# Pair activations computed token by token, multiplied on GpSimd into the summed weights

## Chip, core and metric

The kernel runs on one core of a Trainium2 chip. The metric is device time in microseconds. The engines named here: TensorE (PE, with its weight loads PEld), VectorE (DVE), ScalarE (ACT) and GpSimd (POOL). Each takes its instructions in order and waits on semaphores.

## The reference

Two layers on x of shape (16, 128, 128): 16 tiles of 128 tokens with 128 features, all float32. Each layer is a conditioning part and a feed-forward part with a residual. The change lies in the feed-forward part of layer 0, a product-key memory of 1024 experts:

```python
sim = einsum('pbnhd,hkpd->pbnhk', q, keys)
sx, ix = top_k(sim[0], 8); sy, iy = top_k(sim[1], 8)
all_scores = sx[..., :, None] + sy[..., None, :]
scores, pk = top_k(all_scores, 8)
h = gelu(einsum('bnd,bnhkd->bnhk', x, down_embed[indices]))
h = softmax(scores) * h
out = einsum('bnhk,bnhkd->bnd', h, up_embed[indices])
```

Layer 1 is a mixture of 8 experts of three matrices (256 hidden) and then a mixture of 8 experts of two matrices (512 hidden), on the 128 features of each token.

## The kernel before, in words

The memory is computed densely. For a tile of 128 tokens, `pair_scores` (GpSimd, L401) forms for each of 8 heads all 32x32 sums of key scores; ScalarE masks them (L989) and exponentiates them (L995); `add_weights` (VectorE, L1392) adds the heads, each with its softmax factor, into one array W of 128 tokens x 1024 experts. The activation of every expert for every token, gelu(x . down), is computed by `expert_inputs`: TensorE (L663) multiplies eight blocks of 128 experts, with the block of `downT` as the stationary operand, so that experts lie on partitions; ScalarE (L1003) applies gelu into `act_of[t]`. TensorE's `weights_T` (L673) transposes W into PSUM in eight steps (L681). VectorE's `weigh` (L1479) multiplies these by the activations on their way into `PT` (L1489). `peer_out` (L684) multiplies PT with the `up` matrix, and `add_peer` (L1408) makes the output `x2s` of the layer.

Tiles 0 and 1 are done in another way (TensorE sums their heads, L783); tiles 2 to 15 as told.

Work is staged in turns of two tiles: turn g handles the even tile 2g and the odd tile 2g+1 of the memory, together with layer 1 for the two tiles before. A turn has 16 slots, and each engine's order of instructions in a slot is written out by hand. In slots 4 to 11 layer 1's first mixture runs, one expert a slot: TensorE `hidden1(e+1)`, `outputs1(e-2)`, `hidden2(e)`; VectorE evicts `hidden1(e)` with its ReLU (L1398) and ScalarE `hidden2(e)` (L1041). TensorE's `hidden2(e)` waits for VectorE's `hidden1(e)`, and its `hidden1(7)` waits for VectorE's `hidden1(6)` (L732). The gate of the mixture is worked out on VectorE in slots 4 to 6 (L1432 to L1477; the copy L1462 is `keep_two`). The second mixture runs in slots 12 to 15 and 0 to 3.

The heads of `add_weights` are spread over VectorE's slots by a table: `SUMS` (L1571) in turns 2 to 7, `SUMS_1` (L1573) in turn 1. Entry 1 to 7 is a head of the even tile, 9 to 15 a head of the odd one. Head 0 needs no sum. A sum waits for its predecessor's semaphore. TensorE's `weights_T` for the even tile stands in slot 10, for the odd tile in slot 1 of the next turn. GpSimd's `pair_scores` of head h for the tile after next reuses the buffer of head h and waits for its sum (`h_w`). The buffers of the activations, `G[0]` and `G[1]`, alternate between even and odd tiles.

Of the kernel before, what the change touches and what calls it, by code (L numbers as in the profile page):

```python
# [21 lines left out]
ALU = mybir.AluOpType  # L22
# [3 lines left out]
P = 128  # L26
# [56 lines left out]
def program(nc, xtok, xT, pA, pL, pC, pR, p8, wq, wqT, down, up, w1, w2, w3, f1, f2, out):  # L83
# [7 lines left out]
    with ExitStack() as ctx:  # L91
        def sb(name, shape, dt=F32):
            return ctx.enter_context(nc.sbuf_tensor(name, shape, dt))

        def sem(name):
            return ctx.enter_context(nc.semaphore(name))
# [3 lines left out]
        x1T_all = sb("x1T_all", [P, TOK])  # L100
        downT = sb("downT", [P, NK * NK])
# [81 lines left out]
        W = [W_both[:, 1024 * a:1024 * a + 1024] for a in range(2)]  # L183
# [5 lines left out]
        PT = sb("PT", [P, 1024])  # L189
# [11 lines left out]
        act_of = [HF[n][:, :, :].rearrange("p a n -> p (a n)") for n in range(2)] + [G[n % 2] for n in range(2, B)]  # L201
# [17 lines left out]
        banks = ctx.enter_context(nc.psum_tensor("banks", [P, 8, 512], F32))  # L219

        def bank(n, a=0, b=512):
            return banks[:, n, a:b]
# [25 lines left out]
        topk = sem("topk")  # L248

        t_top, t_ez, t_zs, t_rz = (sem("t_" + n) for n in ("top", "ez", "zs", "rz"))  # L250
        t_Hp, t_G = sem("t_Hp"), sem("t_G")


        t_dg, t_W, t_Tp, t_PT, t_x2p, t_x2, t_xst, t_ssq, t_trp, t_x2T = (
            sem("t_" + n) for n in ("dg", "W", "Tp", "PT", "x2p", "x2", "xst", "ssq", "trp", "x2T"))

        h_S, h_L, h_E, h_w = sem("h_S"), sem("h_L"), sem("h_E"), sem("h_w")
# [15 lines left out]
        def wait(eng, s, value):  # L273

            if not isinstance(value, int) or value > 0:
                eng.wait_ge(s, value)
# [4 lines left out]
        def cols(ap, i, n=P):  # L281
            return ap[:, ds(i * n, n)] if not isinstance(i, int) else ap[:, i * n:(i + 1) * n]

        def tile_of(ap, t):
            if isinstance(t, int):
                return ap[:, t, :]
            return ap[:, ds(t, 1), :].rearrange("p a n -> p (a n)")
# [40 lines left out]
        def _(pool):  # L328
# [60 lines left out]
            def pair_scores(t, a, h):  # L389

                if h == 0:
                    pool.wait_ge(t_simr, t + 1)
                    if t == 0:
                        pool.wait_ge(pe_norm, len(NORM_PE))
                if 2 <= t < 4:
                    pool.wait_ge(t_W, 8 * (t - 2) + h + 1)
                elif h == 0:
                    wait(pool, h_E, 8 * (t - 2) + 1)
                else:
                    wait(pool, h_w, 7 * (t - 4) + h)  # L400
                pool.tensor_tensor(  # L401
                    S[a][h].rearrange("p (i j) -> p i j", i=NK),
                    sim[a][:, h, :].unsqueeze(2).broadcast_to([P, NK, NK]),
                    sim[a][:, PH + h, :].unsqueeze(1).broadcast_to([P, NK, NK]),
                    ALU.add).then_inc(h_S, 1)

            def keep_x2(t, a):
                pool.wait_ge(t_x2, t + 1)
                pool.tensor_copy(tile_of(x_all, t), x2s[a][:, :]).then_inc(t_xst, 1)  # L409
# [8 lines left out]
            def turn(g, peer, new, more=True):  # L418
                t = 2 * g

                def root():
                    pool.wait_ge(g_msq, g)
                    pool.tensor_tensor(rms[:, :], msq[:, :], mhalf[:, 0:2], ALU.pow).then_inc(g_rms, 1)

                if g == 1:
                    root()
                if peer:
                    for h in range(7):
                        pair_scores(t + 1, 1, h)
                if new and g > 1:  # L430
                    keep_x2(t - 1, 1)
                    root()
                if not peer:
                    return
                pair_scores(t + 1, 1, 7)
                if more:
                    for h in range(8):
                        pair_scores(t + 2, 0, h)
                keep_x2(t, 0)

            for t in range(2):
# [2 lines left out]
            for h in range(3):  # L444
                pair_scores(2, 0, h)
            keep_x2(0, 0)
            for h in range(3, 8):
                pair_scores(2, 0, h)
            keep_x2(1, 1)
            for g in range(1, NG - 1):  # L450
                turn(g, True, True)
            turn(NG - 1, True, True, more=False)
            turn(NG, False, True, more=False)


        @block.tensor
        def _(pe):
            def mm(o, l, r, start=True, stop=True):
                return pe.matmul(o, l, r, start=start, stop=stop)  # L459
# [203 lines left out]
            def expert_inputs(t, a, c):  # L663

                if c == 0 and t != 2:
                    pe.wait_ge(t_G, t)
                    wait(pe, t_PT, t - 1)
                b = 4 + c if t == 2 else c
                for k in range(4):
                    m = mm(bank(b, P * k, P * k + P), cols(downT, 4 * c + k), cols(x1T_all, t))  # L670
                m.then_inc(t_Hp, 1)

            def weights_T(t, a):  # L673
                pe.wait_ge(h_w, 7 * t - 7)
                if a == 1:
                    pe.wait_ge(t_G, min(t + 2, B))
                else:
                    pe.wait_ge(e_r2, 4 * t - 2)
                pe.wait_ge(t_PT, t)
                for c in range(8):  # L680
                    m = pe.transpose(bank(c // 4, P * (c % 4), P * (c % 4) + P), W[a][:, P * c:P * c + P], ident[:, :])  # L681
                m.then_inc(t_Tp, 1)
# [100 lines left out]
            def weighted(t, h):  # L783
# [9 lines left out]
                m.then_inc(t_W, 1)  # L793

            expert_inputs(1, 1, 0)
            expert_inputs(1, 1, 1)
            expert_inputs(2, 0, 0)
            expert_inputs(2, 0, 1)
            key_scores(1, 1)
# [16 lines left out]
            def turn(g, peer, new, old, more=True):  # L816
                t, G1, G2 = 2 * g, g - 1, g - 2
                late = new and g > 1
                for s in range(16):
# [14 lines left out]
                    if s == 1 and late:  # L834
                        weights_T(t - 1, 1)
# [22 lines left out]
                    if s == 10 and peer:  # L858
                        weights_T(t, 0)
# [34 lines left out]
        def _(act):  # L894
# [107 lines left out]

            def expert_inputs(t, a):  # L1003
                act.wait_ge(t_Hp, 2 * t + 2)
                if t > 2:
                    act.wait_ge(t_PT, t - 1)
                b = 4 if t == 2 else 0
                act.activation(act_of[t], banks[:, b:b + 2, :].rearrange("p c n -> p (c n)"),
                               ACT.Gelu_apprx_tanh).then_inc(t_G, 1)
# [45 lines left out]
            act.wait_ge(pe_norm, NORM_PE.index("weff0") + 1)  # L1055
            act.activation(weff[:, 0:256], bank(2, 0, 256), ACT.Copy).then_inc(act_norm, 1)
            expert_inputs(0, 0)
            act.wait_ge(pe_norm, NORM_PE.index("sim_bias") + 1)
            act.activation(sim_bias[:, :], bank(7), ACT.Copy).then_inc(act_norm, 1)
            expert_inputs(1, 1)  # L1060
            expert_inputs(2, 0)
            load_table(ACT.Exp, 1)
            exp_top(0, 0)
# [85 lines left out]
        def _(v):  # L1149
# [328 lines left out]

            def weigh(t, a):  # L1479

                b = 0
                if t < 2:
                    b = 2 + 2 * t
                    v.wait_ge(t_W, 8 * t + 8)
                else:
                    v.wait_ge(t_Tp, t - 1)
                v.wait_ge(t_G, t + 1)
                wait(v, t_x2p, t)
                v.tensor_tensor(PT[:, :], banks[:, b:b + 2, :].rearrange("p c n -> p (c n)"), act_of[t],  # L1489
                                ALU.mult).then_inc(t_PT, 1)  # L1490

            def diagonals(t, a, b):
# [22 lines left out]
            def add_expert(Gn, n):  # L1515
# [15 lines left out]
                for a in range(2):  # L1531
# [26 lines left out]
            top_pairs(0)  # L1558
            thresholds(2, 0)
            weigh(0, 0)  # L1560
            add_peer(0, 0)
            key_sums(3, 1)
            top_keys_of(3, 1)
            pair_sums()
            top_pairs(1)
            thresholds(3, 1)
            weigh(1, 1)
            add_peer(1, 1)
            top_sums(2, 0)

            SUMS = {0: [1], 2: [2], 4: [3], 6: [4], 7: [5], 8: [6], 9: [7], 10: [9, 10], 11: [11, 12], 12: [13],  # L1571
                    13: [14], 14: [15]}
            SUMS_1 = {0: [1], 6: [2, 3], 7: [4], 8: [5], 9: [6, 7], 10: [9, 10], 11: [11, 12], 12: [13], 13: [14], 14: [15]}  # L1573
            ADDS = {6: 0, 7: 1, 8: 2, 9: 3, 10: 4, 11: 5, 14: 8, 15: 9}
# [2 lines left out]
            def turn(g, peer, new, old, more=True):  # L1577
                t, G1, G2 = 2 * g, g - 1, g - 2
                late = new and g > 1
                sums = SUMS if late else SUMS_1  # L1580
                slots = list(range(16)) if g != 1 else [4, 5, 0, 6, 1, 7, 2, 8, 3, 9, 10, 11, 12, 13, 14, 15]
                for s in slots:
# [41 lines left out]
                    if s == 2 and late:  # L1624
                        weigh(t - 1, 1)
# [92 lines left out]
```

## Time and profile before

| | us |
|---|---|
| median of 3 runs | 799.05 (798.32 to 799.29) |
| the profiled execution | 798.92 |
| its span, first to last instruction | 797.1 |
| TensorE busy | 762.6 (96%) |
| VectorE busy | 548.3 (69%) |
| ScalarE busy | 574.2 (72%) |
| GpSimd busy | 315.6 (40%) |
| mean granted TensorE clock | 0.989 of full |

The attention part of layer 0 runs until about 145 us, a stretch of set-up and the first tiles until 228, turn 1 until about 276, turns 2 to 7 until about 700, and the rest is the end of layer 1. A busy share is an average over these. Times in a timeline are from the span's start; consecutive matmuls of TensorE overlap in it, so the time that one takes of the engine is read from its start to the start of the next.

### The profile page before, as it was taken

What the parts mean: (1) busy time and instruction counts of PE and PEld (TensorE: products, weight loads), DVE (VectorE), ACT (ScalarE), POOL (GpSimd) and SP (SyncE); (2) the same over time, 40 slices, a digit from 0 to 9 for tenths busy, and PEclk for the clock granted to TensorE, in tenths of its full rate; (3) what the DMA queues carried; (4) which work ended last, traced back from release to release, by engine and by line L of the source; (5) the groups of instructions that cost most, each with busy time, mean ns of one, the idle gap of its engine ahead of it and who ended that gap; (6) DMA issues with size and microseconds to landing.
All of it is one profiled execution on the core that took longest, in us unless ns stands there. A gap on an engine that the chain in (4) does not pass through costs nothing.

```text
span 797.1 us, 14545 instructions
## 1 busy us (share of the span) xinstructions
PE 762.6 (96%) x5186; PEld 681.3 (85%) x5186; DVE 548.3 (69%) x1479; ACT 574.2 (72%) x985; POOL 315.6 (40%) x230
## 2 busy tenths in 40 slices
PE   4999999998976999999999999999999999999998
PEld 3888888887964789899998998999998899899887
DVE  3577667559459967977896697779769765843522
ACT  2667667529978688978887897789789788653343
POOL 2122222049997364516635460763546171000000
PEclk9999999998998999999999999999999999999999
DMA  8930000000000000000000000000000000000000
GB/s 308 340 101 2 1 2 2 1 2 0 2 0 1 2 1 5 4 2 1 8 1 1 1 8 1 1 8 1 2 2 7 1 1 8 1 1 4 5 1 7
DMA packets 11015, 16.85 MB, mean 21 GB/s; under 512 B 664, under 2 KB 6976, under 8 KB 10688
## 3 DMA queue, kind: packets, MB, share of 16 engines
q1 hardware_dynamic: 10944, 15.93, 6.2%
q8 instruction: 42, 0.69, 0.4%
q14 instruction: 29, 0.24, 0.1%
HBM read 14.88 MB, written 1.05 MB: 20 GB/s over the span
## 4 chain that ended last, share of the span: by engine, by line
PE 89%; DVE 6%; issue 3%; ACT 2%; DMA 1%; POOL 0%; DVEq 0%; SPq 0%; ACTq 0%; POOLq 0%
PE banks L459 82%; PE banks L498 4%; PE banks L681 2%; DVE W_both L1392 1%; ACT region L989 1%; DVE acc L1537 1%; DMA region<-in_pC 1%; PE banks L514 0%; DVE W_both L1195 0%; DVE HF L1398 0%; ACT region L995 0%; PE banks L713 0%; DVE pairs L1356 0%; DVE top_keys L1351 0%; DVE PT L1489 0%
## 5 line engine op out<-in xcount | busy, mean ns | idle before, releaser
L401 POOL TENSOR_TENSOR region<-sim 128x1024 f32<-128x1024 f32 x128 | 260.8, 2066 | 99.7 <-DVE top_keys L1349 63.2
L1051 ACT ACTIVATE HF<-banks,lpack 128x256 f32<-128x256 f32 x256 | 105.6, 480 | 55.4 <-PE banks L459 54.5
L989 ACT ACTIVATE region<-region,neg_thr 128x1024 f32<-128x1024 f32 x128 | 143.8, 1153 | 0.0
L1392 DVE SCALAR_TENSOR_TENSOR W_both<-region,rz_rel,W_both 128x1024 f32<-128x1024 f32 x98 | 137.7, 1405 | 1.7
L459 PE MATMUL banks<-HF,w_sb 128*128 128x256 f32 x512 | 124.4, 387 | 7.5 <-DVE HF L1398 7.4
L459 PEld LDWEIGHTS banks<-f_sb,HF 128*128 128x128 f32 x1024 | 123.7, 192 | 3.4
L995 ACT ACTIVATE region<-region,dtop 128x1024 f32<-128x1024 f32 x114 | 125.4, 1142 | 0.0
L459 PE MATMUL banks<-f_sb,HF 128*128 128x128 f32 x1024 | 124.5, 275 | 0.0
L459 PE MATMUL banks<-cT,f_sb 128*128 128x256 f32 x512 | 122.7, 382 | 0.1
L459 PEld LDWEIGHTS banks<-HF,w_sb 128*128 128x128 f32 x512 | 95.2, 194 | 19.8 <-DVE HF L1398 8.5
L459 PEld LDWEIGHTS banks<-cT,f_sb 128*128 128x128 f32 x512 | 92.1, 190 | 16.3 <-issue 2.9
L1041 ACT ACTIVATE H<-banks,lpack 128x256 f32<-128x256 f32 x128 | 53.4, 470 | 49.5 <-PE banks L459 49.5
L459 PE MATMUL banks<-region 128*128 128x128 f32 (+7 forms) x478 | 73.8, 400 | 8.6 <-DMA region<-in_pC 5.3
L409 POOL COPY x_all<-x2s 128x128 f32<-128x128 f32 x16 | 11.6, 723 | 163.7 <-DVE x2s L1408 163.6
L1398 DVE TENSOR_SCALAR HF<-banks,lpack 128x256 f32<-128x256 f32 x128 | 55.8, 476 | 23.9 <-PE banks L459 23.6
L459 PEld LDWEIGHTS banks<-w_sb,H 128*128 128x128 f32 x512 | 66.1, 192 | 6.7 <-ACT H L1041 2.8
L459 PE MATMUL banks<-w_sb,H 128*128 128x128 f32 x512 | 68.7, 277 | 2.1 <-DVE acc L1537 1.0
L1537 DVE SCALAR_TENSOR_TENSOR acc_f<-banks,cw,acc_f 128x128 f32<-128x128 f32 x112 | 34.0, 345 | 50.9 <-PE banks L459 50.1
L459 PE MATMUL banks<-x2T,w_sb 128*128 128x256 f32 x256 | 67.7, 388 | 0.0
L459 PEld LDWEIGHTS banks<-region 128*128 128x128 f32 (+3 forms) x478 | 51.7, 199 | 16.3 <-issue 7.9
L459 PE MATMUL banks<-region,G_both 128*128 128x104 f32 x512 | 62.8, 276 | 0.0
L459 PEld LDWEIGHTS banks<-region,G_both 128*128 128x128 f32 x512 | 59.7, 192 | 0.0
(165 smaller groups left out, 1010.7 us busy)
## 6 DMA issues: line engine op xcount, KB each, us to landing
w_sb<-in_w SPq DMA_DIRECT2D x1, 2048.0 KB, 12.9
f_sb<-in_f SPq DMA_DIRECT2D x1, 2048.0 KB, 15.8
region<-in_wq SPq DMA_DIRECT2D x1, 1024.0 KB, 9.3
region<-in_wqT SPq DMA_DIRECT2D x1, 1024.0 KB, 11.4
w_sb<-in_w SPq DMA_DIRECT2D x1, 1024.0 KB, 8.5
out_x<-acc_f SPq DMA_DIRECT2D x16, 64.0 KB, 1.6
region<-in_pA SPq DMA_DIRECT2D x1, 796.5 KB, 4.3
x1T_all<-in_xT SPq DMA_DIRECT2D x1, 768.0 KB, 8.3
```

The costliest lines, as they stand in the source:

```text
L401: pool.tensor_tensor(S[a][h].rearrange("p (i j) -> p i j", i=NK), sim[a][:, h, :].unsqueeze(2).broadcast_to([P, NK, NK]), sim[a][:, PH + h ...
L409: pool.tensor_copy(tile_of(x_all, t), x2s[a][:, :]).then_inc(t_xst, 1)
L459: return pe.matmul(o, l, r, start=start, stop=stop)
L498: m = pe.transpose(bank(g // FG, P * (g % FG), P * (g % FG) + P), D[q][:, P * g:P * g + P], A("ident"))
L681: m = pe.transpose(bank(c // 4, P * (c % 4), P * (c % 4) + P), W[a][:, P * c:P * c + P], ident[:, :])
L989: act.activation(S[a][h], S[a][h], ACT.Prelu, bias=neg_thr[t % 4][:, h:h + 1], alpha=STEEP).then_inc(h_L, 1)
L995: act.activation(W[a] if h == 0 and t > 1 else S[a][h], S[a][h], ACT.Exp, bias=dtop[t % 4][:, h, 7:8]).then_inc(h_E, 1)
L1041: m = act.activation(H2[e % 2][:, n, :], bank(H2_BANK[e], 256 * n, 256 * n + 256), ACT.Relu, bias=L("b2", 2 * e + n, 2 * e + n + 1))
L1051: m = act.activation(HF[e % 2][:, f, :], bank(2 + b, 256 * (f % 2), 256 * (f % 2) + 256), ACT.Gelu_apprx_tanh, bias=L("bf", 4 * e + f, 4 * ...
L1392: v.scalar_tensor_tensor(W[a], S[a][h], rz_rel[a][:, h:h + 1], W[a], ALU.mult, ALU.add).then_inc(h_w, 1)
L1398: m = v.tensor_scalar(H1[e % 2][:, n, :], bank(H1_BANK[e], 256 * n, 256 * n + 256), L("b1", 2 * e + n, 2 * e + n + 1), 0.0, ALU.add, ALU.max)
L1537: m = v.scalar_tensor_tensor(dst[:, a, :], y, weight, base, ALU.mult, ALU.add)
```

## The change

`expert_inputs` on TensorE takes, for tiles 2 to 15, the tile of x as the stationary operand and 512 columns of `downT` as the moving one: two products, tokens on partitions. The gelu output then has the layout of W. A new step `pair_products` on GpSimd multiplies it into W in place, once the sums are complete, and signals a new semaphore `t_P`. `weights_T` waits for that, and VectorE's `weigh` for these tiles is a copy from PSUM to PT. ScalarE's gelu waits for the GpSimd product of the tile that last used its buffer. On GpSimd the product of the odd tile stands after four of the `pair_scores` of the next odd tile, the one of the even tile between `pair_scores` 6 and 7 of the next even tile. In `SUMS` the even tile's heads 4, 5, 6 and 7 move from slots 6, 7, 8, 9 to slots 5, 6, 7, 8. `SUMS_1` is as it was.

```diff
+            def pair_products(t, a):
+
+                pool.wait_ge(h_w, 7 * t - 7)
+                pool.wait_ge(t_G, t + 1)
+                pool.tensor_tensor(W[a], W[a], act_of[t], ALU.mult).then_inc(t_P, 1)
+
...
                 if peer:
-                    for h in range(7):
+                    for h in range(4):
+                        pair_scores(t + 1, 1, h)
+                if new and g > 1:
+                    pair_products(t - 1, 1)
+                if peer:
+                    for h in range(4, 7):
                         pair_scores(t + 1, 1, h)
...
                 if more:
-                    for h in range(8):
+                    for h in range(7):
                         pair_scores(t + 2, 0, h)
+                pair_products(t, 0)
+                if more:
+                    pair_scores(t + 2, 0, 7)
                 keep_x2(t, 0)
...
-                for k in range(4):
-                    m = mm(bank(b, P * k, P * k + P), cols(downT, 4 * c + k), cols(x1T_all, t))
+                if t > 1:
+                    m = mm(bank(b), cols(x1T_all, t), downT[:, 512 * c:512 * c + 512])
+                else:
+                    for k in range(4):
+                        m = mm(bank(b, P * k, P * k + P), cols(downT, 4 * c + k), cols(x1T_all, t))
                 m.then_inc(t_Hp, 1)
 
             def weights_T(t, a):
-                pe.wait_ge(h_w, 7 * t - 7)
+                pe.wait_ge(t_P, t - 1)
...
-                if t > 2:
+                if t == 3:
                     act.wait_ge(t_PT, t - 1)
+                elif t > 3:
+                    act.wait_ge(t_P, t - 3)
...
-                b = 0
-                if t < 2:
-                    b = 2 + 2 * t
-                    v.wait_ge(t_W, 8 * t + 8)
-                else:
+                wait(v, t_x2p, t)
+                if t > 1:
                     v.wait_ge(t_Tp, t - 1)
+                    v.tensor_copy(PT[:, :], banks[:, 0:2, :].rearrange("p c n -> p (c n)")).then_inc(t_PT, 1)
+                    return
...
-            SUMS = {0: [1], 2: [2], 4: [3], 6: [4], 7: [5], 8: [6], 9: [7], 10: [9, 10], 11: [11, 12], 12: [13],
+            SUMS = {0: [1], 2: [2], 4: [3], 5: [4], 6: [5], 7: [6], 8: [7], 10: [9, 10], 11: [11, 12], 12: [13],
```

## Rows read from the trace of the kernel before

**Rows 1.** Stretches: us, busy (instructions) of each engine, PEclk, DMA share, GB/s.
```profile
250.00:262.00 12.00, 10.10 (x32) 7.86 (x31) 11.97 (x24) 6.71 (x10) 9.57 (x5) 0.64 0.00 0
350.39:420.90 70.51, 70.47 (x461) 63.89 (x461) 55.79 (x158) 58.91 (x97) 34.89 (x19) 1.00 0.01 3
```

**Rows 2.** Waits of TensorE, 230 to 790: total us, times, longest.
```profile
PE banks L459 <- DVE HF L1398: 7.4, 3, 4.4
```

**Rows 3.** Timeline of TensorE: start, us, instruction, count; `key_scores` and `expert_inputs`.
```profile
353.96 1.02 PE L459 MATMUL banks<-weff,x1T_all 128*128 128x512 f32 x2
354.82 1.89 PE L459 MATMUL banks<-cT,f_sb 128*128 128x256 f32 x8
...
358.33 1.95 PE L459 MATMUL banks<-x1T_all,downT 128*128 128x128 f32 x16
360.12 1.89 PE L459 MATMUL banks<-cT,f_sb 128*128 128x256 f32 x8
```

**Rows 4.** Groups of VectorE by form: busy us, mean ns, idle before.
```profile
L1489 DVE TENSOR_TENSOR PT<-banks,G_both 128x1024 f32<-128x1024 f32 x14 | 17.1, 1219 | 1.8 <-PE banks L681 1.8
...
L1339 DVE COPY sim<-banks 128x512 f32<-128x512 f32 x1 | 0.7, 692 | 1.2 <-PE banks L459 1.2
```

**Rows 5.** Timeline of TensorE, turn 3: transposes, `hidden2(4)`, `hidden1(7)`, transposes.
```profile
371.74 1.04 PE L681 MATMUL banks<-ident,W_both 128*128 128x128 f32 x8
...
399.37 1.89 PE L459 MATMUL banks<-HF,w_sb 128*128 128x256 f32 x8
...
404.80 1.03 PE L459 MATMUL banks<-x2T,w_sb 128*128 128x256 f32 x4
...
409.02 1.09 PE L681 MATMUL banks<-ident,W_both 128*128 128x128 f32 x8
```

**Rows 6.** Timeline of VectorE, turn 3: `hidden1(3)`, copy, sums, `hidden1(4)`, `hidden1(6)`.
```profile
391.72 0.88 DVE L1398 TENSOR_SCALAR HF<-banks,lpack 128x256 f32<-128x256 f32 x2
392.51 0.82 DVE L1462 COPY picked<-best 128x4 f32<-128x4 f32 x1
...
394.79 1.28 DVE L1392 SCALAR_TENSOR_TENSOR W_both<-region,rz_rel,W_both 128x1024 f32<-128x1024 f32 x1
395.98 0.87 DVE L1398 TENSOR_SCALAR HF<-banks,lpack 128x256 f32<-128x256 f32 x2
...
400.50 1.84 DVE L1392 SCALAR_TENSOR_TENSOR W_both<-region,rz_rel,W_both 128x1024 f32<-128x1024 f32 x1
402.39 0.88 DVE L1398 TENSOR_SCALAR HF<-banks,lpack 128x256 f32<-128x256 f32 x2
...
404.13 1.28 DVE L1392 SCALAR_TENSOR_TENSOR W_both<-region,rz_rel,W_both 128x1024 f32<-128x1024 f32 x1
```

**Rows 7.** Timeline of GpSimd, turn 3; in brackets the idle time before.
```profile
356.88 14.62 POOL L401 TENSOR_TENSOR region<-sim 128x1024 f32<-128x1024 f32 x7 [9.05 <-DVE top_keys L1349]
...
382.93 10.37 POOL L401 TENSOR_TENSOR region<-sim 128x1024 f32<-128x1024 f32 x5
396.15 1.91 POOL L401 TENSOR_TENSOR region<-sim 128x1024 f32<-128x1024 f32 x1 [2.84 <-DVE W_both L1392]
399.36 1.91 POOL L401 TENSOR_TENSOR region<-sim 128x1024 f32<-128x1024 f32 x1 [1.29 <-DVE W_both L1392]
```

**Rows 8.** Timeline of ScalarE, turn 3: the masks of heads 2 to 4, odd tile.
```profile
375.27 3.22 ACT L989 ACTIVATE region<-region,neg_thr 128x1024 f32<-128x1024 f32 x3
```

**Rows 9.** Timelines of turn 1: TensorE, VectorE and GpSimd.
```profile
265.71 1.09 PE L681 MATMUL banks<-ident,W_both 128*128 128x128 f32 x8
265.73 1.92 POOL L401 TENSOR_TENSOR region<-sim 128x1024 f32<-128x1024 f32 x1 [1.16 <-DVE W_both L1392]
266.88 3.24 DVE L1392 SCALAR_TENSOR_TENSOR W_both<-region,rz_rel,W_both 128x1024 f32<-128x1024 f32 x2
...
271.31 1.13 PE L459 MATMUL banks<-w_sb,H 128*128 128x128 f32 x8 [1.00 <-DVE acc L1537]
...
276.16 0.44 PE L772 MATMUL banks<-ident,acc 128*128 128x128 f32 x2 [0.87 <-DVE acc L1537]
```

More of the change, by code:

```diff
@@ L250, in program @@
         t_top, t_ez, t_zs, t_rz = (sem("t_" + n) for n in ("top", "ez", "zs", "rz"))
-        t_Hp, t_G = sem("t_Hp"), sem("t_G")
+        t_Hp, t_G, t_P = sem("t_Hp"), sem("t_G"), sem("t_P")
         t_dg, t_W, t_Tp, t_PT, t_x2p, t_x2, t_xst, t_ssq, t_trp, t_x2T = (
@@ L1479, in weigh @@
             def weigh(t, a):
-                b = 0
-                if t < 2:
-                    b = 2 + 2 * t
-                    v.wait_ge(t_W, 8 * t + 8)
-                else:
+                wait(v, t_x2p, t)
+                if t > 1:
                     v.wait_ge(t_Tp, t - 1)
+                    v.tensor_copy(PT[:, :], banks[:, 0:2, :].rearrange("p c n -> p (c n)")).then_inc(t_PT, 1)
+                    return
+                v.wait_ge(t_W, 8 * t + 8)
                 v.wait_ge(t_G, t + 1)
-                wait(v, t_x2p, t)
-                v.tensor_tensor(PT[:, :], banks[:, b:b + 2, :].rearrange("p c n -> p (c n)"), act_of[t],
+                v.tensor_tensor(PT[:, :], banks[:, 2 + 2 * t:4 + 2 * t, :].rearrange("p c n -> p (c n)"), act_of[t],
                                 ALU.mult).then_inc(t_PT, 1)
```

## The prediction, as made before the change was run

> **What bounds the kernel now.** I read the stretches first [rows 1]: in one whole steady turn, 350.39 to 420.90, TensorE is busy for 70.47 of 70.51 us at full clock. So in the steady turns nothing costs time unless TensorE gets more work or has to wait, and nothing brings time unless TensorE gets less work. Only 250 to 262, in turn 1, looks different: TensorE idles and its granted clock is 0.64. The table of waits says where TensorE idles after the start-up [rows 2]: mostly for VectorE's "HF" evictions, the ReLUs of `hidden1` (L1398), three times, 7.4 us in all, of which I find every one in turn 1. TensorE is therefore the bound, and the engine nearest to becoming it is VectorE. That makes the timelines of one steady turn, TensorE beside VectorE beside GpSimd, the place to work in; I use turn 3. Turn 2 and turns 4 to 6 repeat it at a shift of 70.5 us.
>
> **1. Two 512-column products for eight 128-column ones.** In a steady turn 16 such instructions (one tile's `expert_inputs`; a float32 product is two instructions) run from 358.33 to the next start at 360.12, 1.79 us a tile. A 512-column product, `key_scores`, runs from 353.96 to 354.82, 0.86 us, so a tile will take 1.72 us [rows 3]. Saved: 0.07 us for each of 14 tiles (2 to 15), about 1.0 us, all on the bounding engine. The arithmetic itself is unchanged, so more is hard to see: below it lies only 0, if the saving is an edge effect.
>
> The Trainium skill, "TensorE: Matmul & The Clock Gate", section "Wait — 56ns, not 53.3ns?", puts a fixed 2.5 ns on each matmul beyond its columns. By it 14 x 12 instructions fewer would give back an estimated 0.4 us in place of my 1.0. The rows give the larger figure, and I take theirs.
>
> **2. VectorE copies instead of multiplying.** The multiplication into PT takes 1219 ns for 1024 columns. The nearest row for a copy out of PSUM is 692 ns for 512 columns [rows 4]; twice that is 1.38 us, and less the fixed part about the same 1.2 us. So VectorE gives up nothing. That work is not shortened, only copied.
>
> **3. GpSimd multiplies.** The product reads and writes 1024 columns of SBUF. Its nearest row is `pair_scores`, 1.91 us for 128x1024 with two inputs [rows 7]. It adds 14 x 1.91 = 27 us to an engine that is 40% busy, but what counts is when.
> - Odd tile: GpSimd runs seven `pair_scores` from 356.88 for 14.62 us. Four of them and the product end at about 367.4. TensorE's transposes of that tile start at 371.74 [rows 5, 7]. Slack 4 us: free. Three `pair_scores` come 2 us later, and their batch ends at 373.4; ScalarE's three instructions for heads 2 to 4 begin at 375.27, so head 4, done at about 369.5, is wanted at 377.3 [rows 8].
> - Even tile: the product is queued between `pair_scores` 6 and 7 and waits for the last sum. Today the last sum ends at 404.13 + 1.28 = 405.4; TensorE transposes at 409.02 [rows 5, 6]. Even unmoved, 405.5 + 1.9 = 407.4 would be in time by 1.6 us. So the new wait is hidden in steady turns, up to a product of 3.5 us.
>
> **4. The even tile's sums, one slot earlier (turns 2 to 7).** The sum for head 4 now stands at the end of slot 5, in front of `hidden1(3)`, not in slot 6. Two things in the rows price that.
>
> First, VectorE instructions with two SBUF inputs, and its tiny SBUF-to-SBUF copies, stand still while a GpSimd instruction runs. The copy of 4 columns (L1462) at 392.51 takes 0.82 us and ends at 393.33; GpSimd's run of five that began at 382.93 ends at 393.30. The sum at 400.50 takes 1.84 instead of 1.28 us; GpSimd's instruction beside it, from 399.36, ends at 401.27 [rows 6, 7]. PSUM evictions such as L1398 are not held up.
>
> Second, the moved sum lands in that same run. It would issue at about 391.7, where `hidden1(3)` issues today, be held until 393.30, and let `hidden1(3)` start at 394.3 (1.0 to 1.1 us after GpSimd is done, as `hidden1(6)` at 402.39 after 401.27). That is 2.65 us later, of which 1.46 us is standing still. Its end releases GpSimd's `pair_scores` for head 4, 394.4 to 396.4, and L1462, issued at 395.1, is held until 396.4: 0.5 us more than today. The rest of the spacing repeats today's (the sum at 400.50, held by 0.6 us, has its counterpart in the sum for head 7). So `hidden1(4)` and `hidden1(6)` both start about 3.05 us later than today.
>
> What was the cover? `hidden1(4)` ends today at 396.85 and TensorE takes it up in the eight instructions at 399.37: cover 2.5 us, short by 0.6. `hidden1(6)` ends at 402.39 + 0.88 = 403.27 and TensorE's `hidden1(7)`, which by L732 waits for it, starts at 404.80: cover 1.5 us, short by 1.57, in which the first 0.6 is contained. After that VectorE waits for TensorE again, so nothing is added by the end of the turn. So 1.57 us a turn. GpSimd's run of 10.37 us comes five times, in turns 2 to 6; turn 7 has none (no further tile to score): 5 x 1.57 = 7.9 us. Bounds for a turn: 0.1 (if the moved sum is not held, the delay is 1.6 against 1.5) and 2.2 (if it is held by another full instruction's remainder). I take 1.57, for the row of L1462 shows something held in just that place.
>
> The Trainium skill, "SBUF — State Buffer", section "SBUF: two separate sides", calls the SBUF port pair that VectorE and GpSimd share an exclusive lock held for the whole instruction; if bandwidth were shared instead, the moved sum would be slowed but not stopped. The row of L1462 agrees with the lock, since four columns can't take 0.82 us at half speed.
>
> **5. Turn 1.** There the sums are not moved. TensorE's transposes start at 265.71, right when the last sum is done; so does a GpSimd instruction of 1.92 us that waited for that sum, at 265.73 [rows 9]. The product takes that place, and TensorE waits until 267.7: 2.0 us. TensorE idles later in the same turn for 1.00 and 0.87 us for VectorE, so of the 2.0 us at least 0.1 to 0.2 stays. But GpSimd's last `pair_scores` moves behind the product, until 269.6, and holds the second of the two sums that start at 266.88 (today only the first is held, 3.24 us for both). That adds up to 1.9 us to VectorE's chain, which is the late one there. I take 1.6 us; bounds 0.2 and 2.0.
>
> **The sum.** Profiled execution 798.92 us (span 797.1, 1.8 around it): 798.92 - 1.0 + 7.9 + 1.6 = 807.4 us. The median of the runs shown, 799.05, lies 0.13 above this execution, inside what I can tell.
>
> **The rivals.**
> - **The sums are not held, or the cover is wider than I read it** (24%). Then only part 1 and turn 1 stay: 798.92 - 1.0 + 0.2 to 1.6, 798.1 to 799.5, with up to 0.2 a turn 800.5. For it: VectorE catches up within each turn, and 1.5 us of cover is close to what one plain sum needs. Against: the held copy in the same place. This is the case on the other side, not slower, and what decides is whether the head-4 sum issues before GpSimd's fifth instruction has ended.
> - **Held once only** (15%): the moved sum is held for part of an instruction, or the copy behind it isn't: 0.2 to 1.0 us a turn, 800.7 to 804.5.
> - **TensorE's clock falls in turn 1** (7%). Ahead of the stretch at 0.64 TensorE had idled 4.4 us at once, its longest wait. With the new 2 us at 265.7 a second fall could come; if the 8 to 10 us of work behind it ran at half speed, 4 to 8 us more than my sum: 811 to 815. Against: the new idle is less than half as long.
> - **The change pays more on TensorE than the rows show** (8%): 168 weight loads go as well, and if the stalls stay out and each tile gave 0.25 us, 14 x 0.25 = 3.5 us: 796.
>
> **How the numbers follow.** My forecast holds 46%: 804.5 to 809.5. Range 799.0 to 809.5: outside it lie the clock (7%), the larger gain (8%) and the low edge of the first rival (3%). Less than 0.2% (1.6 us, about what a measurement of this kernel can tell from no change) is the first rival, 24%. Slower: 46 + 15 + 7 = 68%. Faster: 8%.
>
> **What would show it.** Right: in turns 2 to 6 TensorE has idle time ended by VectorE HF L1398, some 1.5 us a turn; the period of a turn grows from 70.5 to about 71.9; the head-4 sum takes about 2.7 us and L1462 about 1.3. GpSimd's products take 1.9 us, and both steady transposes wait for nothing. In turn 1 the transposes start 2 us after the last sum. Each `expert_inputs` tile takes 1.72 us. Wrong: a steady turn of 70.4 us with a head-4 sum of 1.3 us kills part 4; a product of over 3.5 us would turn the new wait into the bound; a 512-column product far from 0.86 us would upset part 1.

## The result, and the profile after

The changed kernel takes 811.64 us (median of 4 runs, 808.53 to 811.80) against 799.17 us for the kernel before: a ratio of 1.0144, 95% interval 1.0115 to 1.0174. It is slower, as forecast, but by 12.5 us where 8.5 were forecast, and outside the range that ended at 809.5. The profiled execution is 811.69 us, its span 809.9, again 1.8 us around it.

Line numbers have moved: TensorE's L459 is L473, its transposes L681 are L698; VectorE's sums L1392 are L1411, the evictions L1398 are L1417, the copy L1462 is L1481; GpSimd's product is L411.

The page of the changed kernel, part 1, is the first thing to read:

```profile
PE 767.4 (95%) x5018; PEld 669.0 (83%) x5018; DVE 563.2 (70%) x1479; ACT 575.0 (71%) x985; POOL 349.1 (43%) x244
```

168 fewer products and loads on TensorE, and yet it is busy for longer (762.6 before). A busy time that rises while the work falls suggests that part of it ran at a lower clock; the stretches below show where. Then who TensorE waited for from 230 on (total us, times, longest), which answers [rows 2]:

```profile
PE banks L473 <- DVE HF L1417: 12.5, 13, 4.4
PE banks L473 <- ACT cT L1044: 2.5, 2, 2.1
PE banks L698 <- POOL W_both L411: 2.5, 1, 2.5
```

Three waits for VectorE's evictions have become 13: ten new ones, two in each of turns 2 to 6. The product is waited for once, in turn 1. Of the two waits for `cT` one, of 2.05 us, is new and in turn 1; the other, of 0.5 us near the end, was there before. Stretches of the changed kernel (us, busy of each engine, PEclk), three in and around turn 1 and one a whole steady turn, which answer [rows 1]:

```profile
250.00:262.00 12.00, 10.12 (x33) 7.79 (x32) 11.93 (x25) 6.77 (x10) 9.86 (x5) 0.64 0.00 0
262.00:276.00 14.00, 11.49 (x66) 10.15 (x65) 13.58 (x14) 7.34 (x12) 7.11 (x3) 0.87 0.00 1
276.00:288.00 12.00, 9.95 (x47) 7.47 (x47) 6.45 (x20) 9.24 (x16) 1.28 (x1) 0.86 0.00 0
357.64:429.58 71.94, 70.87 (x438) 61.78 (x437) 58.24 (x158) 59.03 (x97) 39.52 (x21) 1.00 0.01 3
```

A steady turn has grown from 70.51 to 71.94 us with TensorE idle for 1.1 of them. And in turn 1 the clock is below full in two stretches more; before, both had 1.00. The chain of work that ended last puts the difference in place. Its long TensorE pieces begin each turn at the same instruction, in the changed kernel:

```profile
285.58 17.84 PE banks L473 x104
...
357.64 17.71 PE banks L473 x104
...
645.37 16.85 PE banks L473 x102
...
714.88 14.28 PE banks L473 x96
```

In the kernel before, the same four stand at 279.88, 350.39, 632.42 and 702.07. So 5.7 us are lost ahead of turn 2 (0.3 of them ahead of turn 1), (645.37 - 285.58) - (632.42 - 279.88) = 7.25 us in turns 2 to 6, -0.14 in turn 7, nothing after: 12.8 us, the whole difference of the two spans. Where the 0.3 us ahead of turn 1 come from stays open.

### The profile page after: what moved, and what is told of

Its sections match the earlier page's. It is cut to its first block, busy times and chain, and to the rows that moved or that the text cites. A ratio compares the mean times of both kernels' runs of the same rounds, so it can differ in the third digit from the quotient of the medians.

```text
span 809.9 us, 14237 instructions
## 1 busy us (share of the span) xinstructions
PE 767.4 (95%) x5018; PEld 669.0 (83%) x5018; DVE 563.2 (70%) x1479; ACT 575.0 (71%) x985; POOL 349.1 (43%) x244
## 4 chain that ended last, share of the span: by engine, by line
PE 75%; DVE 14%; issue 7%; ACT 2%; DMA 1%; POOL 0%; DVEq 0%; SPq 0%; ACTq 0%; POOLq 0%
PE banks L473 68%; PE banks L512 4%; DVE W_both L1411 3%; DVE HF L1417 3%; PE banks L698 2%; DVE acc L1555 1%; DVE picked L1481 1%; ACT region L1006 1%; ACT region L1012 1%; DVE prob L1464 1%; DMA region<-in_pC 1%; PE banks L528 0%; DVE W_both L1214 0%; DVE pairs L1375 0%; DVE acc_f L1555 0%
## 5 line engine op out<-in xcount | busy, mean ns | idle before, releaser
L401 POOL TENSOR_TENSOR region<-sim 128x1024 f32<-128x1024 f32 x128 | 256.1, 2026 | 96.1 <-DVE top_keys L1368 66.5
L1411 DVE SCALAR_TENSOR_TENSOR W_both<-region,rz_rel,W_both 128x1024 f32<-128x1024 f32 x98 | 151.3, 1543 | 1.7
L473 PE MATMUL banks<-HF,w_sb 128*128 128x256 f32 x512 | 125.5, 389 | 9.7 <-DVE HF L1417 9.6
L473 PEld LDWEIGHTS banks<-f_sb,HF 128*128 128x128 f32 x1024 | 123.7, 192 | 3.4
L473 PE MATMUL banks<-f_sb,HF 128*128 128x128 f32 x1024 | 124.5, 275 | 0.0
L473 PE MATMUL banks<-cT,f_sb 128*128 128x256 f32 x512 | 124.2, 386 | 0.1
L473 PEld LDWEIGHTS banks<-HF,w_sb 128*128 128x128 f32 x512 | 95.7, 195 | 23.1 <-DVE HF L1417 11.7
L473 PEld LDWEIGHTS banks<-cT,f_sb 128*128 128x128 f32 x512 | 93.7, 192 | 19.4 <-issue 5.9
L473 PE MATMUL banks<-region 128*128 128x128 f32 (+7 forms) x478 | 73.8, 400 | 8.9 <-DMA region<-in_pC 5.6
L1417 DVE TENSOR_SCALAR HF<-banks,lpack 128x256 f32<-128x256 f32 x128 | 55.6, 475 | 23.4 <-PE banks L473 23.3
L473 PEld LDWEIGHTS banks<-w_sb,H 128*128 128x128 f32 x512 | 67.0, 195 | 5.8 <-ACT H L1060 1.8
L473 PE MATMUL banks<-x2T,w_sb 128*128 128x256 f32 x256 | 68.2, 391 | 2.9 <-DVE HF L1417 2.9
L473 PE MATMUL banks<-w_sb,H 128*128 128x128 f32 x512 | 69.6, 280 | 1.1 <-DVE acc L1552 0.8
L473 PEld LDWEIGHTS banks<-region 128*128 128x128 f32 (+3 forms) x478 | 51.7, 199 | 16.5 <-issue 7.9
L473 PE MATMUL banks<-region,G_both 128*128 128x104 f32 x512 | 62.8, 276 | 0.0
L473 PEld LDWEIGHTS banks<-region,G_both 128*128 128x128 f32 x512 | 59.7, 192 | 0.0
```

Of the source, the lines that this page charges most:

```text
L401: pool.tensor_tensor(S[a][h].rearrange("p (i j) -> p i j", i=NK), sim[a][:, h, :].unsqueeze(2).broadcast_to([P, NK, NK]), sim[a][:, PH + h ...
L1411: v.scalar_tensor_tensor(W[a], S[a][h], rz_rel[a][:, h:h + 1], W[a], ALU.mult, ALU.add).then_inc(h_w, 1)
L1417: m = v.tensor_scalar(H1[e % 2][:, n, :], bank(H1_BANK[e], 256 * n, 256 * n + 256), L("b1", 2 * e + n, 2 * e + n + 1), 0.0, ALU.add, ALU.max)
```

## Where the steady turns lose 1.4 us each

VectorE in turn 3 of the changed kernel, from the point at which it was priced:

```profile
398.85 2.73 DVE L1411 SCALAR_TENSOR_TENSOR W_both<-region,rz_rel,W_both 128x1024 f32<-128x1024 f32 x1
401.50 0.86 DVE L1417 TENSOR_SCALAR HF<-banks,lpack 128x256 f32<-128x256 f32 x2
402.29 1.31 DVE L1481 COPY picked<-best 128x4 f32<-128x4 f32 x1
...
405.05 1.27 DVE L1411 SCALAR_TENSOR_TENSOR W_both<-region,rz_rel,W_both 128x1024 f32<-128x1024 f32 x1
406.25 0.87 DVE L1417 TENSOR_SCALAR HF<-banks,lpack 128x256 f32<-128x256 f32 x2
```

GpSimd and TensorE beside it, in the same turn (the first GpSimd line is its run of five, the two behind it are the fourth and the fifth of these by themselves):

```profile
390.12 10.37 POOL L401 TENSOR_TENSOR region<-sim 128x1024 f32<-128x1024 f32 x5
...
395.73 2.90 POOL L401 TENSOR_TENSOR region<-sim 128x1024 f32<-128x1024 f32 x1
398.58 1.91 POOL L401 TENSOR_TENSOR region<-sim 128x1024 f32<-128x1024 f32 x1
...
401.65 1.91 POOL L401 TENSOR_TENSOR region<-sim 128x1024 f32<-128x1024 f32 x1 [1.16 <-DVE W_both L1411]
...
412.69 2.36 POOL L411 TENSOR_TENSOR W_both<-W_both,G_both 128x1024 f32<-128x1024 f32 x1 [1.16 <-DVE W_both L1411]
```

```profile
407.17 1.99 PE L473 MATMUL banks<-HF,w_sb 128*128 128x256 f32 x8 [0.45 <-DVE HF L1417]
...
413.45 1.13 PE L473 MATMUL banks<-x2T,w_sb 128*128 128x256 f32 x4 [0.58 <-DVE HF L1417]
...
417.77 1.09 PE L698 MATMUL banks<-ident,W_both 128*128 128x128 f32 x8
```

The head-4 sum takes 2.73 us. It is issued at 398.85, 0.27 us after GpSimd's fifth instruction began, and ends 1.09 us after that instruction, which ends at 400.49. It is this one instruction that it waits for, not the run: the head-3 sum, issued at 395.16 in the same run, took 1.70 us, and there GpSimd's fourth instruction was the one held, 2.90 instead of 1.91 us. The head-4 sum's own end releases GpSimd's next scores at 401.65, and those hold the copy L1481 until 403.6. TensorE then idles in front of `hidden2(4)` and in front of `hidden1(7)`; the brackets say 0.45 and 0.58 us. Start to start it is more: against the spacing of the kernel before, 0.62 us is lost at the first place and 0.74 at the second, and 0.1 behind each (the eight products at 407.17 take 1.83 us to the next start where they took 1.73), 1.57 us in all. The transposes at 417.77 wait for nothing: the product that they need ended at 415.05.

**The moved sums alone.**

```diff
-            SUMS = {0: [1], 2: [2], 4: [3], 6: [4], 7: [5], 8: [6], 9: [7], 10: [9, 10], ...
+            SUMS = {0: [1], 2: [2], 4: [3], 5: [4], 6: [5], 7: [6], 8: [7], 10: [9, 10], ...
```

> The kernel before with the moved sums alone; no product on GpSimd, no 512-column products. Theory A: 1.58 us a turn in turns 2 to 6, period 72.1 us, 799.2 + 7.9 = 807.1 us. Rival B: 799.2 us, period 70.5.

Measured 806.58 us against 799.00, ratio 1.0089 (1.0068 to 1.0109): 7.6 us, with neither a product on GpSimd nor a 512-column one. Its period is 72.07 us, 1.56 more than before: theory A.

**The other way round: the changed kernel with its sums back** (the same two lines, exchanged).

> The changed kernel with one part undone: in turns 2 to 7 the even tile's sums stand in their old slots. Theory A, that the moved sums cost the steady turns 1.58 us in each of turns 2 to 6: the period of a turn falls from 71.93 to 70.37 us, no idle time of TensorE before hidden2(4) and hidden1(7), and about 811.6 - 7.9 = 803.7 us. The product of the even tile then starts after the last sum, 1.3 us later than in the changed kernel, and must still end before TensorE's transposes. Rival B, that the GpSimd products cost the steady turns (VectorE held up by them, or TensorE waiting for them): the period stays above 71.5 and the time at 811.

Measured 806.61 us (803.68 to 807.04), ratio to the kernel before 1.0083 (1.0058 to 1.0107). Both theories missed: the period is 70.97 us where they had 70.37 and over 71.5, so 0.97 us a turn came back, not 1.58. TensorE no longer waits for evictions in steady turns, but it has a new wait for VectorE's additions into `acc`; more of that below.

**How much is standing still, how much is plain work.** Two kernels tell it. One moves a single sum:

```diff
-            SUMS = {0: [1], 2: [2], 4: [3], 6: [4], 7: [5], ...
+            SUMS = {0: [1], 2: [2], 4: [3], 5: [4], 7: [5], ...
```

> The kernel before with one sum moved, head 4 from slot 6 to slot 5; heads 5, 6 and 7 stay. Theory A (the moved sum waits until GpSimd's run of five scores has ended, 1.46 us, and the copy L1462 behind it 0.5 us more): hidden1(4) and hidden1(6) later by about 1.9 us, against a cover of 2.5 and 1.5: stall 0.4 us before hidden1(7) alone, in turns 2 to 6, 2.0 us in all, 801.0 us. Rival D (nothing stands still, only one more sum of 1.2 us lies in front): with one sum moved and one gone from the slot behind, hidden1(4) is where it was, no stall, 799.0 us.

Measured 801.35 us, ratio 1.0030 (1.0020 to 1.0040), period 70.94 us, that is 0.43 us a turn where 0.4 was worked out and the rival had none.

The other keeps all four moved, and shortens GpSimd's run:

```diff
+                n = NK // 2 if t > 3 and a == 0 and h in (2, 3) else NK
                 pool.tensor_tensor(
-                    S[a][h].rearrange("p (i j) -> p i j", i=NK),
-                    sim[a][:, h, :].unsqueeze(2).broadcast_to([P, NK, NK]),
+                    S[a][h][:, 0:n * NK].rearrange("p (i j) -> p i j", i=n),
+                    sim[a][:, h, 0:n].unsqueeze(2).broadcast_to([P, n, NK]),
```

> The kernel before with the four moved sums, and GpSimd's scores for heads 2 and 3 of the even tiles from tile 4 on computed for half of the 1024 pairs only (the other half is left out). GpSimd's run of five then ends before the head-4 sum issues. Theory A: the sum takes 1.3 instead of 2.7 us, hidden1(4) and hidden1(6) are later by 1.2 to 1.6 us, against a cover of 2.5 and 1.5: at most 0.1 us a turn is left, 799.0 to 799.6 us. Rival D (the number of sums in front of the evictions is what costs): the stall stays, 806.6 us.

Measured 798.60 us, period 70.75 us: 0.24 us a turn are left (at most 0.1 was expected), of the 1.56 of the moved sums alone (ratio to the kernel before 0.9994, 0.9984 to 1.0003). VectorE in this kernel:

```profile
390.44 1.27 DVE L1393 SCALAR_TENSOR_TENSOR W_both<-region,rz_rel,W_both 128x1024 f32<-128x1024 f32 x1
391.62 0.87 DVE L1399 TENSOR_SCALAR HF<-banks,lpack 128x256 f32<-128x256 f32 x2
392.41 1.31 DVE L1463 COPY picked<-best 128x4 f32<-128x4 f32 x1
```

GpSimd's run of five ends at 390.21 here, before the sum is issued. The head-4 sum is down from 2.73 to 1.27 us, as many sums stand in front of the evictions as in the moved version, and the stall is nearly gone. The copy is still held, by the scores that the sum releases. So it is the standing still behind a GpSimd instruction, not the number of sums. (That the total is even below the periods' account is turn 1, whose tile 4 is shortened too: turn 2 starts 1.6 us sooner.)

The Trainium skill, "SBUF — State Buffer", section "SBUF: two separate sides", has it that the loser of the shared port pair blocks for the whole instruction of the other. By that rule, the trace agrees: the copy ends with GpSimd's instruction (403.60 and 403.56), the head-4 sum ends 1.09 us after one, most of the 1.27 us that a sum takes by itself, and GpSimd's own fourth instruction is held behind the head-3 sum.

**The 512-column products alone**, in the kernel before:

```diff
-                for k in range(4):
-                    m = mm(bank(b, P * k, P * k + P), cols(downT, 4 * c + k), cols(x1T_all, t))
+                if t > 1:
+                    m = mm(bank(b), cols(x1T_all, t), downT[:, 512 * c:512 * c + 512])
+                else:
+                    for k in range(4):
+                        m = mm(bank(b, P * k, P * k + P), cols(downT, 4 * c + k), cols(x1T_all, t))
```

> The kernel before with the 512-column products alone, for tiles 2 to 15. VectorE still multiplies, but the activations now lie token by token while the transposed weights lie expert by expert, so the pairing of the two is left out of this kernel's result. Theory A: each tile's products take 1.72 instead of 1.79 us, period 70.37 instead of 70.51 us, 1.0 us in all: 799.0 - 1.0 = 798.0 us. Rival: no gain of TensorE at all, 799.0 us and a period of 70.51.

Measured 798.72 us, ratio 0.9997 (0.9987 to 1.0006). The period is 70.37 us, shorter by the 0.14 us a turn of two tiles that was worked out. The medians differ by 0.3 us, and the interval holds both the 1.0 us expected and none; the gain is read from the period in the trace alone.

## Where turn 1 loses 5.4 us

TensorE in the changed kernel, which answers [rows 9]:

```profile
268.43 1.36 PE L698 MATMUL banks<-ident,W_both 128*128 128x128 f32 x8 [2.47 <-POOL W_both L411]
...
271.29 2.51 PE L473 MATMUL banks<-HF,w_sb 128*128 128x256 f32 x8
...
281.71 0.61 PE L473 MATMUL banks<-lpack,cT 128*128 128x8 f32 x4 [2.05 <-ACT cT L1044]
282.17 3.20 PE L473 MATMUL banks<-cT,f_sb 128*128 128x256 f32 x8
```

The two levels of the clock, each in a stretch of its own after its wait:

```profile
269.20:272.40 3.20, 3.20 (x14) 3.02 (x13) 3.10 (x3) 0.00 (x0) 2.02 (x1) 0.50 0.00 0
272.60:282.60 10.00, 7.90 (x50) 6.09 (x49) 7.40 (x15) 7.97 (x11) 1.28 (x1) 1.00 0.00 1
282.80:286.10 3.30, 3.30 (x10) 2.57 (x9) 2.09 (x10) 1.53 (x4) 0.00 (x0) 0.50 0.00 0
```

And ScalarE at the end of the same turn, in the changed kernel and then in the kernel before:

```profile
273.83 0.84 ACT L1060 ACTIVATE H<-banks,lpack 128x256 f32<-128x256 f32 x2 [6.66 <-PE banks L473]
274.56 2.19 ACT L1006 ACTIVATE region<-region,neg_thr 128x1024 f32<-128x1024 f32 x2
276.65 1.14 ACT L1012 ACTIVATE W_both<-region,dtop 128x1024 f32<-128x1024 f32 x1
277.69 2.18 ACT L1012 ACTIVATE region<-region,dtop 128x1024 f32<-128x1024 f32 x2
279.88 1.28 ACT L990 ACT_TABLE_LOAD   x1
...
281.29 0.37 ACT L1044 ACTIVATE cT<-banks 128x256 f32<-128x256 f32 x1
```

```profile
269.46 0.84 ACT L1041 ACTIVATE H<-banks,lpack 128x256 f32<-128x256 f32 x2 [2.55 <-PE banks L459]
...
276.91 0.37 ACT L1025 ACTIVATE cT<-banks 128x256 f32<-128x256 f32 x1
```

Followed down the turn, against the kernel before and net of 0.3 us from ahead of it: the transposes are 2.4 us later (the product takes 2.35 us, not 1.9). `hidden2(7)` is 3.5 us later: between the two the same work took 2.86 instead of 1.82 us, at a lower clock. The products that need cT are 4.1 us later. And the work from there to 287.51 takes 5.80 instead of 4.34 us, again at a lower clock. That is 2.4 + 1.0 + 0.6 + 1.5 = 5.5 us, within 0.1 of what the chain of work gives.

ScalarE is the link that my sum lacks. Its last eviction of the first mixture waits for `hidden2(7)`; behind it stand 7.5 us of masks, exponentials and a table load without a gap, and then the copy of cT, which TensorE waits for. In the kernel before, the same eviction ran at 269.46 and the copy at 276.91, straight behind the same work, and it ended 0.05 us before TensorE took it up at 277.33. The slack of TensorE that I counted on, 1.00 and 0.87 us of waits for VectorE [rows 9], was there and was used up, but it was not the path. VectorE's chain was priced rightly: the two sums behind the product take 5.13 us for 3.24, the 1.9 us foreseen.

**Turn 1 as before, the rest as changed.** Tile 2 keeps its eight products, VectorE's multiplication, and transposes that wait for the sums:

```diff
-                if t > 1:
+                if t > 2:
                     m = mm(bank(b), cols(x1T_all, t), downT[:, 512 * c:512 * c + 512])
...
-                pe.wait_ge(t_P, t - 1)
+                if t == 2:
+                    pe.wait_ge(h_w, 7)
+                else:
+                    pe.wait_ge(t_P, t - 2)
...
-                pair_products(t, 0)
+                if g > 1:
+                    pair_products(t, 0)
```

> The changed kernel with tile 2 alone (turn 1) done as before: eight 128-column products, VectorE multiplies into PT, TensorE's transposes wait for the sums alone. Theory A: turn 1 lost 5.4 us to the product in front of the transposes and to what followed from it (TensorE's clock, ScalarE's late copy of cT); all of it comes back, 811.6 - 5.4 = 806.2 us, and the granted clock of turn 1 after 262 us is full again. Rival C: the loss of turn 1 comes from the rest of the change (other instruction order, start-up), and at most 2.4 us, the bare wait for the product, come back: 809.2 us.

Measured 806.05 us (ratio to the kernel before 1.0083, 1.0066 to 1.0100) against the changed kernel's 811.64, so 5.6 us came back where 5.4 were expected and the rival had 2.4, and the clock from 262 on is full:

```profile
262.00:276.00 14.00, 11.53 (x76) 9.56 (x74) 13.48 (x18) 10.27 (x14) 3.82 (x2) 1.00 0.01 2
276.00:288.00 12.00, 11.82 (x68) 9.67 (x69) 8.37 (x36) 8.70 (x21) 2.89 (x2) 1.00 0.00 0
```

**A shorter product, in the same place.** From the kernel with its sums back (806.61 us):

```diff
-                pool.tensor_tensor(W[a], W[a], act_of[t], ALU.mult).then_inc(t_P, 1)
+                n = 256 if t == 2 else 1024
+                pool.tensor_tensor(W[a][:, 0:n], W[a][:, 0:n], act_of[t][:, 0:n], ALU.mult).then_inc(t_P, 1)
```

> The changed kernel with the sums in their old slots (which ran at 806.6 us), and the product of tile 2 on GpSimd taken over 256 of its 1024 columns (the others are left without it). The wait and its order in every queue stay, its length falls from 2.35 to about 0.6 us. Theory A (turn 1 pays first for the length of TensorE's wait and then again for the clock that falls after it): TensorE waits 0.7 us before the transposes, its clock stays at full speed, and nearly all of turn 1's 5 us come back: 802 us. Rival E (the wait alone, and ScalarE's late copy, no clock): 1.8 us come back, 804.8 us. Rival F (order, not length): 806.6 us.

Measured 803.52 us, with a spread of 801.52 to 805.22 (ratio to the kernel before 1.0056, 1.0039 to 1.0073): by the medians 3.1 us came back, where theory A had 4.6 and rival E 1.8. The trace is of a run of 802.03 us. In it TensorE waits 0.86 us ahead of the transposes, the stretch 262 to 276 is back at full clock, the wait for cT in turn 1 is gone, and turn 2 starts at 280.87 instead of 285.44: 4.6 us for a product of 0.73 instead of 2.35 us, shorter by 1.6. So the length of the wait is what turn 1 pays, and it pays more than the length. How much more varies from run to run: two of the six took 805.2 us, and why they gained less than the one traced, no trace shows.

**Less work on ScalarE**, from the same kernel:

```diff
-                act.activation(W[a] if h == 0 and t > 1 else S[a][h], S[a][h], ACT.Exp,
+                n = 32 if t == 4 and h in (1, 2) else 1024
+                dst = W[a] if h == 0 and t > 1 else S[a][h]
+                act.activation(dst[:, 0:n], S[a][h][:, 0:n], ACT.Exp,
```

> The changed kernel with the sums in their old slots (which ran at 806.6 us), and two of ScalarE's exponentials of turn 1, heads 1 and 2 of tile 4, taken over 32 of 1024 columns (the rest is left out), 2.0 us less work between its last eviction of the first mixture and the copy of cT. Theory A (in turn 1 TensorE's late start reaches cT through ScalarE, which has no slack there): TensorE's wait of 2.05 us for cT goes, and 2.0 us come back, 804.6 us, up to 1.4 more if TensorE's clock then stays up behind it. Rival G (ScalarE's lateness is covered by TensorE's own): 806.6 us.

Measured 803.66 us (803.10 to 804.51; ratio to the kernel before 1.0064, 1.0046 to 1.0082), 2.9 us less for 1.7 us less work (the two exponentials take 0.52 instead of 2.18 us; 2.0 was expected); turn 2 starts at 282.57. TensorE's wait for cT in turn 1 is 0.4 us. Its wait for the product is still 2.4 us and the clock from 262 to 276 still 0.86, but from 276 to 288 it is 1.00:

```profile
262.00:276.00 14.00, 11.55 (x66) 10.16 (x65) 13.58 (x14) 7.18 (x11) 7.10 (x3) 0.86 0.00 1
276.00:288.00 12.00, 11.61 (x65) 8.78 (x65) 8.08 (x23) 9.67 (x21) 1.28 (x1) 1.00 0.01 1
```

So the two waits each have a stretch of lower clock behind them, and each goes with its own wait. ScalarE's lateness and the clock behind it are both real terms, as theory A had it.

## What the moved sums were covering

**Both undone together** (the edits of the two kernels above in one):

> Both of the others together: sums in their old slots and tile 2 done as before; tiles 3 to 15 keep the 512-column products and the product on GpSimd. Theory A: 799.2 minus 13 tiles x 0.07 us = 798.3 us, period 70.37 us. If the GpSimd products cost anything in steady turns (rival B), it is above 799.2.

Measured 801.52 us, ratio 1.0028 (1.0018 to 1.0038): 3.2 us above what I expected, period 70.98 us. VectorE, TensorE and GpSimd in turn 3 of this kernel:

```profile
406.93 4.53 DVE L1415 SCALAR_TENSOR_TENSOR W_both<-region,rz_rel,W_both 128x1024 f32<-128x1024 f32 x2
```

```profile
417.51 0.44 PE L793 MATMUL banks<-ident,acc 128*128 128x128 f32 x2 [0.39 <-DVE acc L1564]
```

```profile
405.15 2.37 POOL L411 TENSOR_TENSOR W_both<-W_both,G_both 128x1024 f32<-128x1024 f32 x1 [1.16 <-DVE W_both L1415]
407.47 2.90 POOL L401 TENSOR_TENSOR region<-sim 128x1024 f32<-128x1024 f32 x1
```

The product is in time for the transposes by itself, as I had said. What I had not asked is who else it stands beside. The two sums of slot 10 now run beside the product and the scores behind it and take 4.53 us instead of 2.66; the additions into `acc` behind them come late, and TensorE's transposes of `acc` wait. With the sums moved, as the change has them, this wait is gone, at the price of the longer stall earlier in the turn.

**One odd sum later**, from that kernel:

```diff
-            SUMS = {..., 9: [7], 10: [9, 10], 11: [11, 12], 12: [13],
+            SUMS = {..., 9: [7], 10: [9], 11: [10, 11], 12: [12, 13],
```

> The kernel with both parts undone (even sums in their old slots, tile 2 as before; it ran at 801.5 us), and in turns 2 to 7 one odd sum moved back by a slot: heads 1, then 2 and 3, then 4 and 5 in slots 10, 11, 12, so that one sum less stands in front of VectorE's additions that TensorE's transposes of acc wait for. Theory A: the 0.6 us a turn that are left there (period 70.98 us) come from the two sums of slot 10, held up by the product and the scores behind it on GpSimd; with one sum fewer ahead the period is 70.37 us and the time 801.5 - 3.0 = 798.5 us, level with the kernel before. Rival: the wait stays, 801.5 us.

Measured 798.76 us against 798.73, ratio 1.0004 (0.9994 to 1.0014), period 70.37 us: the whole of the steady loss is gone, and what is left is the gain of 0.14 us a turn from the products, too little for the times to show. With the sums placed so and tile 2 done as before, the change is free, not profitable.

**The same in turn 1:**

> The same, with the same move in turn 1 too, where TensorE waits twice for VectorE's additions, 1.00 and 0.87 us. Both waits go; ScalarE's copy of cT then sets the pace within about 0.6 us: 0.5 to 1.9 us less than the one above, about 797.4 us. Rival: ScalarE takes all of it, 798.5 us.

Measured 799.40 us, ratio 1.0007 (0.9997 to 1.0017): no gain. In its trace TensorE waits 1.26 us for cT in turn 1, where the kernel above had no such wait, and ScalarE's copy of cT runs at 277.30, where it ran at 277.16: ScalarE takes what VectorE gives, as the rival had it.

## What makes the product 2.4 us

> Which property makes GpSimd's product last 2.36 us where the scores, with as many columns, last 1.91. The kernel at 801.5 us (sums in their old slots, tile 2 as before), with the product of four even tiles altered, so that those tiles' memory output is left out of what the kernel computes: tile 4 adds instead of multiplying; tile 6 takes the activations from 32 columns, repeated; tile 8 reads the activations twice and writes W, so it is not in place; tile 10 reads two repeated stretches of 32 columns, like the scores, and multiplies. Tile 12 stays. Theory H (two inputs that are read through cost more than repeated ones): 2.36 for tiles 4, 8 and 12, 1.91 for tile 10, in between for tile 6. Theory I (writing where it reads): 1.91 for tiles 8 and 10, 2.36 for 4, 6 and 12. Theory J (multiplying instead of adding): 1.91 for tile 4 alone.

GpSimd's products of the even tiles 4, 6, 8, 10 and 12, in order:

```profile
335.27 2.37 POOL L417 TENSOR_TENSOR W_both<-W_both,G_both 128x1024 f32<-128x1024 f32 x1 [1.16 <-DVE W_both L1430]
...
406.24 2.38 POOL L419 TENSOR_TENSOR W_both<-W_both,G_both 128x1024 f32<-128x1024 f32 x1 [1.16 <-DVE W_both L1430]
...
477.23 1.90 POOL L421 TENSOR_TENSOR W_both<-G_both 128x1024 f32<-128x1024 f32 x1 [1.16 <-DVE W_both L1430]
...
547.81 1.92 POOL L423 TENSOR_TENSOR W_both<-G_both 128x1024 f32<-128x1024 f32 x1 [1.16 <-DVE W_both L1430]
...
618.40 2.37 POOL L425 TENSOR_TENSOR W_both<-W_both,G_both 128x1024 f32<-128x1024 f32 x1 [1.16 <-DVE W_both L1430]
```

Adding costs what multiplying costs, and a repeated input saves nothing. The two that don't write where they read take 1.9 us. That fits theory I, with one thing open: in those two both inputs also come from one array, and in the slow ones from two. That was not separated.

## Why the prediction was right or wrong

- **The bound** (TensorE in steady turns, VectorE next): right.
- **Part 1, the products**: right, 0.14 us a turn measured, as worked out.
- **Part 2, the copy**: right, 1.21 us.
- **Part 3, GpSimd's product**: mis-sized, 2.36 us for 1.91, and 3.34 us for the odd tiles of turns 2 to 7, where a sum of VectorE, issued ahead of it, ends 1.1 us into it (373.24 in turn 3, the product from 372.12). In the steady turns TensorE's wait for it is hidden all the same. "Free" was wrong as a general statement: with the sums in their old places it costs 0.6 us a turn through VectorE's sums in slot 10.
- **Part 4, the moved sums**: right in mechanism, in both places of the stall and in size: the head-4 sum 2.73 us for 2.65, L1462 1.31 for about 1.3, the period 71.94 for about 71.9, and 7.25 us net of the products in turns 2 to 6, where the sum had 7.9 - 0.7. The step from the delay to the stall was loose by 0.1 us: 2.65 + 0.5 is 3.15, not 3.05, and 3.05 less the cover of 1.53 is 1.52, not 1.57.
- **Part 5, turn 1**: the step that failed. I took 1.6 us, bounded by 0.2 and 2.0, and 5.4 came. The bounds rested on a product of 1.9 us and on TensorE's and VectorE's slack; the product is 0.45 us longer and the whole wait for it stayed (2.4 us), the path ran through ScalarE, which has no slack (0.6 us more), and the clock fell twice (2.5 us). I had the clock as a rival, with 7% and 811 to 815 us. That 811.6 lies there is partly luck: one fall of 4 to 8 us was priced, two came with 2.5 us in sum, and the rest of the excess is the wait that the sum let shrink to 1.6 us and that stayed whole and grew to 3.0.
- **The range** ended at 809.5 because turn 1 had at most 2.0 us in it. With 5.4 us in place of 1.6 the sum would have given 811.2.

## What to carry to other kernels

Where VectorE and GpSimd both work in SBUF, price a moved VectorE instruction by what GpSimd is doing at its new place: the same sum took 1.27 us beside an idle GpSimd and 2.73 when it was issued just after one of its instructions began; a sum of the same size issued later in an instruction of the same run took 1.70. Before calling a new wait in a ragged stretch covered, follow each engine's queue behind it to the next thing that TensorE needs; the slack of two engines says nothing on the third. And to a wait of TensorE there, allow for the clock: it cost 1.0 and 1.5 us behind waits of 2.5 and 2.1 us here, though not behind every wait of that length.

## What was not expected of the hardware

After waits of 2.47 and 2.05 us TensorE's granted clock went to 0.50, 1.2 GHz of 2.4, and came back to 1.00 in each case (the stretches in the section on turn 1), with a busy engine on both sides; matmuls of 256 columns went from 1.9 to 3.2 us for eight. After one of 0.86 us it stayed at 1.00. But the length of the wait doesn't decide alone: in the kernel with the moved sums alone, in the one with turn 1 as before and in the one with both turns' sums later, TensorE waited 2.7 to 2.9 us for an eviction until about 258, and its clock was 1.00 from 254 to 276. What decides it is not shown here. One of the changed kernel's four runs was 3 us shorter than the others (808.53), as was one of the kernel with its sums back (803.68 among 806.5 to 807.0). Each had the highest mean clock of its four, 0.989 where the others had 0.981 to 0.987, which fits a clock that was low for less time; no trace was kept of them.

GpSimd's two-input instruction over 1024 columns took 2.37 us when it wrote over one of its inputs (two arrays), and 1.90 us when it didn't (both inputs from one array); which of the two differences counts is not separated.
